# A sorted segment sum by one-hot matrices: three of eight regular one-hots made by GpSimd

## The chip, the cores and the metric

The kernel runs on one core of a Trainium2 chip. The metric is the device time of one execution in microseconds; for the kernel before, three runs were timed. A core has five engines that run side by side and wait for each other through semaphores: TensorE (PE), VectorE (DVE), ScalarE (ACT), GpSimd (POOL) and SyncE (SP), which here only issues DMAs.

## The reference, cut to what matters

One layer of a graph network over 50,000 nodes of 128 values and 25,000 edges, whose targets `dst` are sorted (and crowd at the low node numbers, since they are drawn as 50,000 u²):

```python
h = jnp.maximum(_layernorm(x, axis=-1), 0.0)
msg_input = jnp.concatenate([h[src], h[dst], edge_attr], axis=-1)
x1 = jax.nn.relu(msg_input @ Wm1 + bm1)
messages = jax.nn.relu(x1 @ Wm2 + bm2)
agg = jax.ops.segment_sum(messages, dst, num_segments=N)
u = jax.nn.relu(jnp.concatenate([h, agg], axis=-1) @ Wu1 + bu1)
out = x + h + (u @ Wu2 + bu2)
```

## The kernel before, in words

**Two parts.** The first part (to about 532 us) normalises the nodes, gathers the two ends of each edge and makes `msgs`, the messages already multiplied by their half of `Wu1`, in tiles of 128 edges. It also leaves two scratch tensors in HBM, the rest of the hidden input (`hu_scratch`) and x + h + bias (`xh_scratch`). The second part, which the change is about, goes over 98 groups of 512 nodes. For each group it sums the messages that end in it, and writes 512 rows of the result.

**The sum of a group.** A table `ranges` tells, for each group g, the range of edge tiles that touch it: at least two, so there are always two regular tiles (the first, n = 0, and the second, n = 1) and, in the early groups, some more. For each tile the kernel needs a one-hot matrix `hot` of 128 edges by 512 nodes (1 where `node` equals `dst` minus the group's base), and the messages split in two parts that TensorE takes exactly: `high` (ScalarE rounds it) and `low` = message - `high` (GpSimd subtracts). TensorE adds `low` x `hot` and `high` x `hot` into the group's bank (L871, L872).

**Who makes the one-hots.** The program text goes through the groups in fours; `slot` is g mod 4, and slot s uses the buffers 2s and 2s + 1 of `hot`, `high` and `low` for its regular tiles. VectorE makes the one-hot of the first tile of every group, and of all further tiles (L769). The one-hot of the second tile comes from ScalarE in slots 0, 1 and 2, in two activations: `dist` = |node - place| (L832) and `hot` = relu(1 - `dist`) (L839). For that GpSimd makes `place`, a column of `dst` minus base (L753). In slot 3 VectorE makes both. So of eight regular one-hots of four groups VectorE makes five and ScalarE three.

**Order on each engine.** Each engine runs its own instruction stream in program order; `EdgeTiles.visit` (L165) has the order within a group: the ranges of the next four groups are loaded into registers in slot 0 (L171), then comes what stands in `before` (GpSimd's place), then the first regular tile, the further tiles, and the second regular tile.
- ScalarE, group g: `high` of the first tile, of further tiles, `dist`, `high` of the second, `hot`, and then `u_t` = relu(`hu_i`) of group g - 2 (L856). It begins a group when the sum of g - 4 is done.
- GpSimd, group g: `place` (L753, slots 0 to 2), then a `low` part (L739) for each tile, as the `high` parts come.
- VectorE, group g: its one-hots, then `hu_i` += the sum of g - 2 (L792), then `xh_o` = output bank + `xh_i` of g - 4 (L803).
- TensorE, group g: the output product of g - 3 (L905), then the sums of g.
- SyncE: loads of `hu_i` and `xh_i` up to four groups ahead (L131, L134) and the store of the result (L717), 256 KB each.

## Time and profile before

| What | Value |
|---|---|
| Median of three runs | 800.0 us (798.3 to 801.7) |
| Profiled execution | 800.3 us |
| Its span, first to last instruction | 798.4 us |
| Granted TensorE clock | 0.998 |
| Busy over the span: PE, DVE, ACT, POOL | 87%, 85%, 79%, 71% |
| Second part, from the first sum to the end | about 532 to 798 us |

The times of single instructions are those of the one profiled execution. The busy shares above are means over both parts, which have different limits: GpSimd's 71% is mostly the issuing of gathers in the first part, and says nothing of the room that it has in the second. For the change the stretches of the second part have to be read one by one.

### The profile page before, as it was taken

What the parts mean: (1) busy time and instruction counts of PE and PEld (TensorE: products, weight loads), DVE (VectorE), ACT (ScalarE), POOL (GpSimd) and SP (SyncE); (2) the same over time, 40 slices, a digit from 0 to 9 for tenths busy, and PEclk for the clock granted to TensorE, in tenths of its full rate; (3) what the DMA queues carried; (4) which work ended last, traced back from release to release, by engine and by line L of the source; (5) the groups of instructions that cost most, each with busy time, mean ns of one, the idle gap of its engine ahead of it and who ended that gap; (6) DMA issues with size and microseconds to landing.
All of it is one profiled execution on the core that took longest, in us unless ns stands there. A gap on an engine that the chain in (4) does not pass through costs nothing.

```text
span 798.4 us, 18682 instructions
## 1 busy us (share of the span) xinstructions
PE 694.5 (87%) x3154; PEld 414.7 (52%) x3155; DVE 676.5 (85%) x2269; ACT 630.5 (79%) x1434; POOL 563.7 (71%) x784
## 2 busy tenths in 40 slices
PE   0398999999988888888888888889999999999997
PEld 0244444444444444434444444445778778776765
DVE  2798888988888888888888888769999998998886
ACT  0588888888888888888888888756788888888886
POOL 7777777777777777777777777639777656655542
PEclk9999999999999999999999999999999999999999
DMA  5466666666666666666666665450579999999998
GB/s 153 119 212 217 215 217 220 228 223 216 217 217 208 199 205 213 213 209 201 199 203 210 213 217 184 149 211 14 172 228 271 335 339 330 368 346 348 360 355 292
DMA packets 99727, 184.56 MB, mean 231 GB/s; under 512 B 15101, under 2 KB 16512, under 8 KB 99700
## 3 DMA queue, kind: packets, MB, share of 16 engines
q1 hardware_dynamic: 46628, 81.69, 30.5%
q10 hardware_dynamic: 40528, 76.89, 26.9%
q0 software_dynamic: 12544, 25.72, 12.0%
q14 instruction: 21, 0.17, 0.1%
q8 instruction: 6, 0.10, 0.0%
HBM read 107.25 MB, written 76.98 MB: 231 GB/s over the span
## 4 chain that ended last, share of the span: by engine, by line
DMA 38%; PE 20%; issue 19%; DVE 7%; POOL 6%; ACT 4%; DVEq 2%; ACTq 2%; SPq 1%; POOLq 1%
DMA xg<-x_in,ends_all 36%; PE bank L871 7%; PE bank L905 5%; POOL xg L318 5%; PE bank L872 5%; DVE hot L769 2%; ACT zn L506 1%; DVE xg L446 1%; DVE hu_i L792 1%; DVE xh_o L803 1%; ACT high L823 1%; ACT dist L832 1%; POOL low L739 1%; DVEq L171 1%; DMA hu_i<-hu_scratch 1%
## 5 line engine op out<-in xcount | busy, mean ns | idle before, releaser
L318 POOL DMA_INDIRECT xg<-x_in,ends_all x392 | 392.9, 1002 | 119.9 <-DMA xg<-x_in,ends_all 104.5
L739 POOL TENSOR_TENSOR low<-msgs,high 128x128 fp32r<-128x128 f32 x303 | 153.0, 520 | 88.1 <-ACT high L823 84.2
L506 ACT ACTIVATE zn<-xn,shift,rstd 128x128 f32<-128x128 f32 x392 | 160.5, 483 | 2.0 <-DVE shift L423 1.8
L871 PE MATMUL bank<-hot,low 128*128 128x512 f32 x303 | 136.1, 449 | 10.3 <-DVE hot L769 3.9
L769 DVE TENSOR_SCALAR hot<-node,dst_f,minus_base 128x512 fp32r<-128x512 f32 x229 | 131.3, 619 | 15.6 <-PE bank L872 11.7
L381 DVE BATCH_NORM_STATS2 bn<-xg 128x6 f32<-128x128 f32 x392 | 80.5, 278 | 51.8 <-DMA xg<-x_in,ends_all 51.8
L872 PE MATMUL bank<-hot,high 128*128 128x512 f32 x303 | 119.6, 395 | 0.0
L609 PE MATMUL bank<-ident,xg 128*128 128x128 f32 x392 | 64.5, 288 | 54.8 <-DVE xg L446 54.8
L625 PE MATMUL bank<-ht,w_uh 128*128 128x512 f32 x196 | 106.1, 623 | 2.9 <-ACT ht L525 1.9
L446 DVE TENSOR_SCALAR xg<-xg,rstd,shift 128x128 f32<-128x128 f32 x392 | 107.3, 357 | 0.1
L905 PEld LDWEIGHTS bank<-w_out,u_t 128*128 128x128 f32 x784 | 99.1, 191 | 15.4 <-issue 7.1
L905 PE MATMUL bank<-w_out,u_t 128*128 128x128 f32 x784 | 105.5, 278 | 0.7 <-ACT u_t L856 0.7
L823 ACT ACTIVATE high<-msgs 128x128 fp32r x303 | 81.8, 299 | 20.6 <-issue 10.3
L609 PEld LDWEIGHTS bank<-ident,xg 128*128 128x128 f32 x392 | 41.5, 141 | 106.2 <-DVE xg L446 105.8
L372 DVE BATCH_NORM_STATS2 bn<-xn 128x6 f32<-128x128 f32 x392 | 94.2, 276 | 0.0
L871 PEld LDWEIGHTS bank<-hot,low 128*128 128x128 f32 x303 | 56.9, 188 | 54.4 <-issue 29.5
L525 ACT ACTIVATE ht<-bank,b_u 128x512 f32<-128x512 f32 x98 | 66.5, 678 | 15.5 <-PE bank L625 14.6
L618 PE MATMUL bank<-ident,zn 128*128 128x128 f32 x392 | 52.9, 279 | 29.0 <-ACT zn L506 29.0
L792 DVE TENSOR_TENSOR hu_i<-bank,hu_i 128x512 f32<-128x512 f32 x98 | 66.8, 681 | 6.3 <-PE bank L872 3.9
L856 ACT ACTIVATE u_t<-hu_i 128x512 f32<-128x512 f32 x98 | 60.6, 619 | 12.4 <-DVE hu_i L792 12.3
L803 DVE TENSOR_TENSOR xh_o<-bank,xh_i 128x512 f32<-128x512 f32 x98 | 66.6, 679 | 2.4 <-PE bank L905 1.2
L432 DVE TENSOR_TENSOR xh_o<-zn,xn 128x512 f32<-128x512 f32 x98 | 67.3, 688 | 0.0
(72 smaller groups left out, 1001.8 us busy)
## 6 DMA issues: line engine op xcount, KB each, us to landing
hu_i<-hu_scratch SPq DMA_DIRECT2D x98, 256.0 KB, 4.4
xh_i<-xh_scratch SPq DMA_DIRECT2D x98, 256.0 KB, 4.4
out<-xh_o SPq DMA_DIRECT2D x97, 256.0 KB, 4.4
hu_scratch<-ht ACTq DMA_DIRECT2D x48, 512.0 KB
xh_scratch<-xh_o ACTq DMA_DIRECT2D x48, 512.0 KB
xn<-x_in ACTq DMA_DIRECT2D x44, 512.0 KB, 3.7
xg<-x_in,ends_all POOLq DMA_INDIRECT x392, 2.8
edge<-edge_t_in ACTq DMA_DIRECT2D x45, 64.0 KB
```

The lines of the kernel that those rows point to most:

```text
L318: pool.indirect_dma_start(xg[:, slot, t, :], None, x, bass.IndirectOffsetOnAxis(ap=ends_all[:, s, t:t + 1], axis=0), engine_sem=s_made).th ...
L372: return dve.bn_stats(bn[:, slot % 2, 8 + t, :], xn[:, slot, t, :])
L446: ins = dve.tensor_scalar(xg[:, slot, t, :], xg[:, slot, t, :], rstd[:, half, t:t + 1], shift[:, half, t:t + 1], ALU.mult, ALU.add)
L506: ins = act.activation(zn[:, slot % 2, t - 8, :], xn[:, slot, t - 8, :], ACT.Relu, bias=shift[:, slot % 2, t:t + 1], scale=rstd[:, slot % ...
L609: ins = pe.transpose(p_tr[q][:, j * P:(j + 1) * P], xg[:, slot, 4 * q + j, :], ident[:])
L625: pe.matmul(p_hu[:], w_uh[:], ht[:, slot % 2, 2 + n, :], start=True, stop=True).then_inc(s_hus, 1)
L739: return pool.tensor_tensor(low[:, at, :], msgs[:, k, :], high[:, at, :].bitcast(F32), ALU.subtract)
L769: return dve.tensor_scalar(hot[:, at, :], node[:], dst_f[:, bass.ds(k, 1)], minus_base[:, bass.ds(g, 1)], ALU.subtract, ALU.is_equal)
L823: return act.activation(high[:, at, :], msgs[:, k, :], ACT.Copy)
L871: pe.matmul(to, low[:, at, :], hot[:, at, :], start=start, stop=False, skip_group_check=True)
L872: return pe.matmul(to, high[:, at, :], hot[:, at, :], start=False, stop=stop, skip_group_check=True)
L905: ins = pe.matmul(to[:, j * D:(j + 1) * D], u_t[:, slot % 2, j * P:(j + 1) * P], w_out[:], start=True, stop=True)
```

## The change

Slots 0 and 1 stay as they are (first one-hot by VectorE, second by ScalarE). In slot 2 the second one-hot goes from ScalarE to GpSimd. In slot 3 both one-hots go from VectorE to GpSimd. VectorE now makes three of the eight, GpSimd three and ScalarE two. GpSimd makes a one-hot in one instruction from `node` and a column `place`; it needs two places in slot 3, so `place` has five columns. GpSimd's places in slots 2 and 3 also wait for the sum of g - 4 and for its own one-hots of the round before; a wait for the transposes of the ends is put at the start of its second part.

```diff
-        place, ones = sb("place", [P, 4]), sb("ones", [P, 1])
+        place, ones = sb("place", [P, 5]), sb("ones", [P, 1])
...
+                pool.wait_ge(s_tre, 2 * STEPS)
...
                     def regular(k, at, n):
                         pool.wait_ge(s_hi, 2 * g + n + 1)
+                        if n == 0 and slot > 1:
+
+                            pool.wait_ge(s_rel_p, 3 * use + (1 if slot == 2 else 3))
                         part(k, at).then_inc(s_lo, 1)
+                        if n == 0 and slot > 1:
+                            onehot(2 * slot + 1)
...
-                    def place_of(k):
-                        if slot < 3:
+                    def onehot(at):
+                        pool.tensor_scalar(hot[:, at, :], node[:], place[:, at - 3:at - 2], None, ALU.is_equal
+                                           ).then_inc(s_hot_p, 1)
+
+                    def places_of(k):
+                        def place_of(k, at):
+                            return pool.tensor_tensor(place[:, at:at + 1], dst_f[:, bass.ds(k, 1)],
+                                                      minus_base[:, bass.ds(g, 1)], ALU.add)
+
+                        if slot < 2:
                             if at_least(g, 4):
-                                pool.wait_ge(s_dist, 3 * use + slot - 2)
-                            pool.tensor_tensor(place[:, slot:slot + 1], dst_f[:, bass.ds(k, 1)],
-                                               minus_base[:, bass.ds(g, 1)], ALU.add).then_inc(s_rel, 1)
+                                pool.wait_ge(s_dist, 2 * use + slot - 1)
+                            place_of(k, slot).then_inc(s_rel, 1)
+                            return
+                        if at_least(g, 4):
+                            pool.wait_ge(s_agg, g - 3)
+                            pool.wait_ge(s_hot_p, 3 * use)
+                        if slot == 3:
+                            place_of(k - 1, 3).then_inc(s_rel_p, 1)
+                            pool.wait_ge(s_rel_p, 3 * use + 2)
+                            place_of(k, 4).then_inc(s_rel_p, 1)
+                            onehot(6)
+                        else:
+                            place_of(k, 2).then_inc(s_rel_p, 1)
...
                     def regular(k, at, n):
-                        if n == 0:
+                        if n == 0 and slot < 3:
                             onehot(k, at).then_inc(s_hot, 1)
-                        elif slot == 3:
-                            onehot(k, at).then_inc(s_hot_v, 1)
...
-                        if n == 1 and slot < 3:
+                        if n == 1 and slot < 2:
...
-                        if n == 0:
-                            pe.wait_ge(s_hot, g + 1)
-                        elif slot < 3:
-                            pe.wait_ge(s_hot_a, 3 * use + slot + 1)
+                        if n == 0 and slot < 3:
+                            pe.wait_ge(s_hot, 3 * use + slot + 1)
+                        elif n == 1 and slot < 2:
+                            pe.wait_ge(s_hot_a, 2 * use + slot + 1)
                         else:
-                            pe.wait_ge(s_hot_v, use + 1)
+
+                            pe.wait_ge(s_hot_p, 3 * use + (1 if slot == 2 else 2 + n))
```

How it moves the rows of GpSimd at the start of slot 3 in the loop. Before:

```order
L172 ISA
L739 ISA
L739 TENSOR_TENSOR low<-msgs,high 128x128
L177 REGISTER_ALU
L177 COMPARE_AND_BRANCH
L156 ISA
```

and now:

```order
L172 ISA
L762 ISA
L762 TENSOR_TENSOR place<-dst_f,minus_base 128x1
L767 REGISTER_ALU
L762 ISA
L762 TENSOR_TENSOR place<-dst_f,minus_base 128x1
L757 TENSOR_SCALAR hot<-node,place 128x512
L744 ISA
L747 REGISTER_ALU
L741 ISA
L741 TENSOR_TENSOR low<-msgs,high 128x128
L757 TENSOR_SCALAR hot<-node,place 128x512
```

Two places and a one-hot stand ahead of the first low part of slot 3, and a second one-hot behind it, ahead of everything else in the slot.

ScalarE at the end of slot 2 in the loop (the `else` of further tiles ends with the branch of L179). Before:

```order
L179 UNCONDITIONAL_BRANCH
L829 REGISTER_ALU
L832 ACTIVATE dist<-node,place 128x512
L823 ISA
L823 ACTIVATE high<-msgs 128x128
L839 ACTIVATE hot<-dist,ones 128x512
L853 REGISTER_ALU
L856 ACTIVATE u_t<-hu_i 128x512
```

and now:

```order
L179 UNCONDITIONAL_BRANCH
L846 ISA
L846 ACTIVATE high<-msgs 128x128
L876 REGISTER_ALU
L879 ACTIVATE u_t<-hu_i 128x512
L172 ISA
```

The `dist` and the `hot` around the second high part are gone; nothing else moves.

## Rows read from the trace of the kernel before

**Rows 1.** Busy us (xinstructions) of PE, PEld, DVE, ACT, POOL; clock, DMA share, GB/s

```profile
571.00:595.00 24.00, 22.99 (x119) 17.01 (x119) 23.88 (x43) 17.09 (x48) 18.74 (x39) 1.00 0.76 221
608.00:639.00 31.00, 30.22 (x182) 25.52 (x181) 30.95 (x55) 27.11 (x69) 20.88 (x49) 1.00 0.98 323
684.00:789.00 105.00, 100.81 (x585) 75.03 (x584) 93.41 (x159) 90.61 (x220) 55.27 (x136) 1.00 1.00 353
```

**Rows 2.** Waits, 661 to 787 us: who waited for whom, us, times, longest

```profile
POOL low L739 <- ACT high L823: 45.2, 75, 0.9
```

**Rows 3.** ScalarE's `dist` in four stretches: ns min/median/max, first and last start

```profile
L832 ACT ACTIVATE dist<-node,place x10: 722/724/727, 542.3 to 590.5; 128x512 f32<-128x512 f32 x10
...
L832 ACT ACTIVATE dist<-node,place x13: 707/713/724, 590.5 to 632.6; 128x512 f32<-128x512 f32 x13
...
L832 ACT ACTIVATE dist<-node,place x10: 707/711/723, 632.6 to 661.3; 128x512 f32<-128x512 f32 x10
...
L832 ACT ACTIVATE dist<-node,place x43: 705/710/726, 661.3 to 785.9; 128x512 f32<-128x512 f32 x43
...
  POOL place L753: 11.7, 15
```

**Rows 4.** GpSimd's low parts (L739) alone in the same four stretches, columns as rows 1

```profile
542.31:590.47 48.16, 38.65 (x72) 1.00 0.45 132
590.47:632.58 42.11, 25.70 (x56) 1.00 0.92 290
632.58:661.30 28.72, 15.42 (x33) 1.00 0.98 332
661.30:785.87 124.57, 61.62 (x124) 1.00 1.00 350
```

**Rows 5.** ScalarE in order of time, one late round: start us, us [idle before]

```profile
733.30 0.72 ACT L832 ACTIVATE dist<-node,place 128x512 f32<-128x512 f32 x1 [1.04 <-POOL place L753]
...
736.28 0.71 ACT L839 ACTIVATE hot<-dist,ones 128x512 fp32r<-128x512 f32 x1
736.89 0.62 ACT L856 ACTIVATE u_t<-hu_i 128x512 f32<-128x512 f32 x1
737.41 0.29 ACT L823 ACTIVATE high<-msgs 128x128 fp32r x1
...
739.56 0.49 ACT L823 ACTIVATE high<-msgs 128x128 fp32r x2
...
742.02 0.72 ACT L832 ACTIVATE dist<-node,place 128x512 f32<-128x512 f32 x1 [0.75 <-POOL place L753]
```

**Rows 6.** GpSimd in order of time, the same round

```profile
736.55 0.46 POOL L739 TENSOR_TENSOR low<-msgs,high 128x128 fp32r<-128x128 f32 x1 [0.35 <-ACT high L823]
736.96 0.19 POOL L753 TENSOR_TENSOR place<-dst_f,minus_base 128x1 f32 x1
737.88 0.46 POOL L739 TENSOR_TENSOR low<-msgs,high 128x128 fp32r<-128x128 f32 x1 [0.73 <-ACT high L823]
...
740.02 1.22 POOL L739 TENSOR_TENSOR low<-msgs,high 128x128 fp32r<-128x128 f32 x2 [0.87 <-ACT high L823]
741.80 0.19 POOL L753 TENSOR_TENSOR place<-dst_f,minus_base 128x1 f32 x1 [0.56 <-issue]
```

**Rows 7.** VectorE in order of time: one-hots beside low parts, and alone

```profile
535.69 5.46 DVE L769 TENSOR_SCALAR hot<-node,dst_f,minus_base 128x512 fp32r<-128x512 f32 x9
...
601.35 0.99 DVE L769 TENSOR_SCALAR hot<-node,dst_f,minus_base 128x512 fp32r<-128x512 f32 x2
602.26 0.68 DVE L792 TENSOR_TENSOR hu_i<-bank,hu_i 128x512 f32<-128x512 f32 x1
```

**Rows 8.** GpSimd's groups by line and shape: xcount | busy us, mean ns | idle

```profile
L302 POOL IOTA xh_o<- 128x512 int32 x1 | 0.6, 567 | 0.0
...
L324 POOL TENSOR_SCALAR_AFFINE_SELECT ident<-ident 128x128 f32<-128x128 f32 x1 | 0.3, 304 | 0.0
...
L306 POOL MEMSET eps<- 128x1 f32 x1 | 0.1, 94 | 0.0
```

More of the change, by code:

```diff
@@ L113, in build @@
         s_ldx = [sem(f"xh_loaded{i}") for i in range(4)]
-        s_hot, s_hot_x = sem("first_onehots_ready"), sem("more_onehots_ready")
-        s_hot_a, s_hot_v = sem("last_onehots_by_scalar"), sem("last_onehots_by_vector")
-        s_rel, s_dist, s_one = sem("places_in_group_ready"), sem("distances_ready"), sem("ones_made")
+        s_hot, s_hot_x = sem("first_onehots_by_vector"), sem("more_onehots_ready")
+        s_hot_a, s_hot_p = sem("last_onehots_by_scalar"), sem("onehots_by_gpsimd")
+        s_rel, s_rel_p, s_dist, s_one = sem("places_for_scalar"), sem("places_for_gpsimd"), sem("distances_ready"), sem("ones_made")
         s_hi, s_hi_x = sem("high_parts_ready"), sem("more_high_parts_ready")
@@ L747, in more @@
                         part(k, at).then_inc(s_lo_x, 1)
-                    def place_of(k):
-                        if slot < 3:
-                            if at_least(g, 4):
-                                pool.wait_ge(s_dist, 3 * use + slot - 2)
-                            pool.tensor_tensor(place[:, slot:slot + 1], dst_f[:, bass.ds(k, 1)],
-                                               minus_base[:, bass.ds(g, 1)], ALU.add).then_inc(s_rel, 1)
+                    def onehot(at):
[6 more added lines that the diff above has]
+                        if slot < 2:
+                            if at_least(g, 4):
+                                pool.wait_ge(s_dist, 2 * use + slot - 1)
[11 more added lines that the diff above has]
+                            place_of(k, 2).then_inc(s_rel_p, 1)
                     if not at_least(g, 1):
                         pool.memset(ones[:], 1.0).then_inc(s_one, 1)
-                    tiles.visit(g, slot, regular, more, place_of)
+                    tiles.visit(g, slot, regular, more, places_of)
                 run_steps(pool, GROUPS, 4, GROUPS, 4, body)
@@ L825, in regular @@
                     def regular(k, at, n):
-                        count = 3 * use + slot + 1
-                        if n == 1 and slot < 3:
+                        count = 2 * use + slot + 1
+                        if n == 1 and slot < 2:
                             act.wait_ge(s_rel, count)
@@ L834, in regular @@
                         part(k, at).then_inc(s_hi, 1)
-                        if n == 1 and slot < 3:
+                        if n == 1 and slot < 2:
                             act.wait_ge(s_dist, count)
```

## The prediction

> **What bounds the kernel now.** The stretch that the change touches runs from about 532 us to the end. I first read the engines' busy times by stretch [rows 1]. Up to 639 us VectorE is busy without a break and DMA has room; in 684 to 789 us it is busy 93.4 of 105 us, ScalarE 90.6, GpSimd 55.3, and the DMA engines show a share of 1.00. The granted clock is 1.00 throughout, so TensorE's price per instruction stays out of it. GpSimd looks like the engine with room: it waits for ScalarE's high parts [rows 2].
>
> A share says nothing of who follows whom, so next I read when ScalarE starts the `dist` of slot 0, once in four groups [rows 3]. From 661.3 to 785.9 us lie 43 of them, 14 rounds of four groups (three `dist` each, and the last start is again a slot 0): 124.6 / 14 = 8.90 us a round. The same division gives 28.7 / 3 = 9.57 (632.6 to 661.3), 42.1 / 4 = 10.5 (590.5 to 632.6) and 48.2 / 3 = 16.1 (542.3 to 590.5). The low parts per round are 124 / 14 = 8.9, 11, 14 and 24 [rows 4]; eight of them are regular.
>
> What sets the 8.90 is a ring of two engines. In a late round [rows 5, 6]: `dist` of slot 0 starts at 733.30; ScalarE works through slots 0, 1 and 2 and starts slot 3's high parts at 739.56 (6.26 us on); GpSimd turns these into low parts from 740.02 (0.46 later) in 1.22 us, loads the ranges, makes slot 0's place at 741.80, and `dist` starts at 742.02, having waited 0.75 us for that place. Sum: 6.26 + 0.46 + 1.78 + 0.22 = 8.72, the round's own time. ScalarE waits for the place in all late rounds, 11.7 us in 15 waits [rows 3]. Neither engine is full; the round is a chain that passes through both, and half idle time on GpSimd is its turn to wait.
>
> **The change part by part.** VectorE loses both one-hots of slot 3. Its one-hot costs 0.60 us start to start where GpSimd works beside it (5.46 us for 9) and 0.455 where it doesn't (601.35 to 602.26 for two) [rows 7]. That is 1.1 us a round. It is worth something only up to about 639 us, where VectorE is never idle.
>
> ScalarE loses slot 2's `dist` and `hot`, 0.61 us each start to start: 1.22 us a round. Of the ring this takes a piece: after `dist` of slot 0, slot 2's first high part starts at 737.41 [rows 5], 4.11 us on, and from there GpSimd is what the ring runs through.
>
> GpSimd gains three one-hots and two places a round and gives nothing up. A place is 0.19 [rows 6]. **X, the price of a 128x512 one-hot on GpSimd, is in no row.** Start to start an instruction costs 0.04 to 0.05 less than its row says (low part 736.55, next instruction 736.96, row 0.46). Lower bound: the IOTA of 128x512, which reads nothing, 0.57, so 0.52. Upper bound: a two-input subtraction costs 0.46 at 128 columns and 0.19 at one, 0.27 per 128 columns, so 0.19 + 4 x 0.27 - 0.05 = 1.22. Nearest is the row with one input and a comparison, AFFINE_SELECT of 128x128, 0.304 [rows 8]. With a fixed part of 0.09 (MEMSET of one column) it scales to 0.95, with 0.19 to 0.65; less 0.05, 0.60 to 0.90. I take the middle, 0.75, and 0.05 for the share of SBUF that it must wait for, since VectorE's one-hot beside GpSimd shows such a wait: **X = 0.80**. The Trainium skill (GPSIMD Engine Reference, Elementwise side-by-side cycle accounting) has 769 ns measured for 512 elements in a tight loop with little work per element; the ring's sum would then be 0.1 us a round less. No run here shows that figure yet.
>
> The ring after the change, for four groups of two tiles: from `dist` of slot 0 to slot 2's high part 4.11; to its low part 0.47 (737.41 to 737.88); low part 0.42; one-hot X; low part 0.42; first place of slot 3 with the wait for its own end, 0.34; second place 0.20; one-hot X; low part 0.42; one-hot X; low part 0.42; place of slot 0 and hand-over 0.22. That is 7.02 + 3X = **9.42 us**. The load of the ranges, which stands open today as 0.56 us of idle time ahead of slot 0's place [rows 6], I cost at nothing: it is the sequencer's, and an X and a low part are queued in front of it; without that cover it costs up to 0.56. ScalarE's saved 1.22 us buys nothing in this sum, since ScalarE now waits for the place of slot 0 until GpSimd is through slot 3. Nor can GpSimd begin slot 2 earlier: its one-hots there stand behind a low part that needs ScalarE's high part.
>
> Tiles beyond eight lengthen the ring only where they stand in it: in slot 0 nothing, in slot 1 a high part of 0.2, in slots 2 and 3 a low part of 0.42 (0.5 beside VectorE's one-hots). The mean is 0.26 to 0.30 each. By stretch:
> 661.3 to 785.9: 9.42 + 0.9 x 0.26 = 9.64 against 8.90, x14 = +10.4.
> 632.6 to 661.3: 9.42 + 3 x 0.26 = 10.2 against 9.57, x3 = +1.9.
> 590.5 to 632.6: 9.42 + 6 x 0.3 = 11.2 against 10.5, x4 = +2.8; the first of these rounds holds most tiles and is not longer, so +2.5.
> 542.3 to 590.5: the ring (9.42 + 16 x 0.33 = 14.7) lies under 16.1. VectorE bounds; it gives back 1.1 a round and loses some 0.6 to one-hots of GpSimd in its way, -0.5 in two rounds; the first has no room on GpSimd: -1.0.
> Sum +13.8 us. The profiled execution took 800.3 us (span 798.4) and the median of the three runs is 800.0: 800.3 + 13.8 = **814 us**. Everything ahead of 532 us is untouched; the added wait for the transposes of the ends is over before GpSimd gets its first high part. TensorE now waits for GpSimd's one-hots in slots 2 and 3, but it waits there for the low parts of the same engine anyhow; the last one-hot of slot 3 is ready one low part ahead of its own low part, so no price of its own. GpSimd's added waits for `s_agg` g-3 have nothing behind them that isn't already held by the high parts, since ScalarE waits for the same.
>
> DMA doesn't decide: at 9.6 us a round for four groups it moves less per microsecond than in the 8.9 us of today.
>
> **Rivals.** (a) X is near its lower bound. At 0.55 the late round is 7.02 + 1.65 + 0.23 = 8.90, just today's; below it DMA at its share of 1.00 keeps 8.8 to 8.9. This is the break-even point. With X = 0.52 the total is -2 to 0: 798 to 801. For it: the IOTA row. Against it: AFFINE_SELECT, already half of that at a quarter of the columns. (b) The other side, faster: VectorE is the only bound up to 639 us and the ring has slack that I don't see (ScalarE's saved 1.22 us shortens a path through `u_t`, which in the early rounds is late). Then the seven rounds up to 639 us give back what VectorE loses, up to 1.1 each, until TensorE (30.2 of 31 us busy [rows 1]) stops it: at 0.8 each, -5.6 us: 795. It needs X under 0.6 and half of the one-hots outside VectorE's way. (c) X is dear, near the two-input price, 1.1 to 1.2: 3 x 0.35 x 21 rounds = +22 on top: 836. (d) The one-hots block VectorE for their whole length. Rows show some sharing: 0.60 against 0.455 [rows 7] beside a low part whose row is 0.46 long. If each of three X stops VectorE for 0.8 us, it loses 2.4 where it saves 1.1: +1.3 a round in the five or six rounds that VectorE bounds, and X grows by its waiting: 822. The Trainium skill (SBUF — State Buffer, Who interferes with whom) states just this, an exclusive lock for the whole instruction, taken by whoever issues first. The trace agrees in that both engines slow down together (one-hots 0.60 and low parts about as long in the row of nine); how long a one-hot on GpSimd holds VectorE, no row shows.
>
> **How the numbers follow.** Forecast, X from 0.7 to 0.95, 806 to 820: 0.50. Same mechanism at X from 0.6 to 0.7, 802 to 806: 0.12. (a) 0.12. (b) 0.08. (c) 0.09. (d) 0.09. The range reaches from the upper half of (a), 799, past (d) to the lower part of (c), 828. Over 0.5% is 4 us, about what a measurement of this kernel can tell from no change: slower (over 804) 0.50 + 0.08 + 0.18 = 0.76; same 0.16; faster (under 796) 0.08.
>
> **What would show it.** In the changed kernel's trace: X start to start in the one-hot rows on GpSimd (0.7 to 0.95); the starts of slot 0's `dist` 9.4 to 9.8 us apart late, and ScalarE's wait for the place grown from 0.75 us (today's late round) to about 2.5 us a round, or the same time spent waiting ahead of `u_t`; GpSimd without a gap from slot 2's first low part to slot 0's place; VectorE no longer full before 639 us; DMA's share under 1.00 late. Rounds that stay at 8.9 us with such an X would mean that the chain is cut somewhere, and that I took for a ring what was two engines that only happened to meet.

## The result: 885.7 us, 11% slower, and six times the forecast loss

The changed kernel takes 885.67 us in the median of four runs (882.62 to 890.13), the kernel before, run beside it on the same chip, 800.85 us (798.3 to 802.71). The ratio is 1.107 (95% interval 1.102 to 1.112). Slower was forecast, but by 14 us, not by 85; the time lies far outside the range of 799 to 828 us. Ratios in this text leave out executions over 1.5% longer than the fastest of the same kernel.

The profiled execution took 890.13 us, with a span of 888.3. The page's busy times, and the group of the new one-hots with its durations (ns min/median/max, first and last start):

```profile
PE 726.4 (82%) x3154; PEld 444.0 (50%) x3155; DVE 665.9 (75%) x2221; ACT 605.9 (68%) x1386; POOL 684.4 (77%) x904
...
L757 POOL TENSOR_SCALAR hot<-node,place 128x512 fp32r<-128x512 f32 x72 | 118.2, 1642 | 0.0
...
L757 POOL TENSOR_SCALAR hot<-node,place x72: 1556/1564/1841, 557.2 to 873.6; 128x512 fp32r<-128x512 f32 x72
```

Most of the one-hots on GpSimd are 1.56 us long, 1.53 start to start: twice the X = 0.80 of the forecast, and above its upper bound of 1.22. The mean of all 72 is 1.64, since some are stretched by VectorE's one-hots (see the rivals below). The other engines now have room where they had none. Busy us of PE, PEld, DVE, ACT and POOL, then clock, DMA share and GB/s, of the stretches of [rows 1] and of the late part:

```profile
571.00:595.00 24.00, 20.43 (x100) 16.29 (x99) 18.60 (x32) 13.55 (x39) 20.37 (x37) 0.93 0.55 165
608.00:639.00 31.00, 25.60 (x125) 20.28 (x124) 24.32 (x41) 16.71 (x46) 25.78 (x45) 0.89 0.64 198
700.00:880.00 180.00, 140.43 (x739) 110.66 (x738) 111.87 (x175) 98.79 (x247) 142.89 (x249) 0.92 0.82 258
```

VectorE, full up to 639 us before, works 24.32 of 31 us. Late, DMA has fallen from a share of 1.00 to 0.82. In that late stretch GpSimd is the busiest engine, and even it is idle for a fifth of the time. So there again a chain, and not a full engine, sets the pace. The late `dist` of ScalarE, with what it waited for (compare the last stretch of [rows 3]; there are now two `dist` a round, so 28 steps are 14 rounds), and the waits from 700 to 880 us (us in total, times, longest), which answer to [rows 2]:

```profile
L855 ACT ACTIVATE dist<-node,place x29: 705/721/725, 705.3 to 875.8; 128x512 f32<-128x512 f32 x29
...
  POOL place L762: 51.6, 15
```

```profile
ACT dist L855 <- POOL place L762: 51.6, 15, 4.8
PEld bank L894 <- POOL low L741: 47.9, 43, 2.1
...
POOL low L741 <- ACT high L846: 33.3, 54, 0.8
```

170.5 / 14 = 12.18 us a round against 8.90. ScalarE's wait for slot 0's place has gone from 11.7 to 51.6 us in 15 waits, 3.4 us each. One late round with eight tiles, ScalarE's part of it first, then GpSimd's (start us, us, [idle before]); it answers to [rows 5, 6]:

```profile
804.19 0.72 ACT L855 ACTIVATE dist<-node,place 128x512 f32<-128x512 f32 x1 [4.82 <-POOL place L762]
...
808.30 0.49 ACT L846 ACTIVATE high<-msgs 128x128 fp32r x2
...
815.89 0.72 ACT L855 ACTIVATE dist<-node,place 128x512 f32<-128x512 f32 x1 [3.87 <-POOL place L762]
```

```profile
808.85 0.46 POOL L741 TENSOR_TENSOR low<-msgs,high 128x128 fp32r<-128x128 f32 x1 [0.81 <-ACT high L846]
809.29 1.57 POOL L757 TENSOR_SCALAR hot<-node,place 128x512 fp32r<-128x512 f32 x1
810.82 0.46 POOL L741 TENSOR_TENSOR low<-msgs,high 128x128 fp32r<-128x128 f32 x1
811.23 0.20 POOL L762 TENSOR_TENSOR place<-dst_f,minus_base 128x1 f32 x1
811.60 0.19 POOL L762 TENSOR_TENSOR place<-dst_f,minus_base 128x1 f32 x1 [0.18 <-POOL place L762]
811.76 1.56 POOL L757 TENSOR_SCALAR hot<-node,place 128x512 fp32r<-128x512 f32 x1
813.29 0.45 POOL L741 TENSOR_TENSOR low<-msgs,high 128x128 fp32r<-128x128 f32 x1
813.72 1.56 POOL L757 TENSOR_SCALAR hot<-node,place 128x512 fp32r<-128x512 f32 x1
815.25 0.45 POOL L741 TENSOR_TENSOR low<-msgs,high 128x128 fp32r<-128x128 f32 x1
815.67 0.19 POOL L762 TENSOR_TENSOR place<-dst_f,minus_base 128x1 f32 x1
```

Read as the forecast's ring: 4.11 (804.19 to 808.30) + 0.55 + 0.44 + **1.53** + 0.41 + 0.37 + 0.16 + **1.53** + 0.43 + **1.53** + 0.42 + 0.22 = 11.70 us, the round's own time. The forecast's 7.02 + 3X gives 11.61 with this X. In such a late round the structure was right link by link.

### The profile page after: what moved, and what is told of

It is laid out like the page before. It is cut to its first block, busy times and chain, and to the rows that moved or that the text cites. A ratio compares the mean times of both kernels' runs of the same rounds, so it can differ in the third digit from the quotient of the medians.

```text
span 888.3 us, 18754 instructions
## 1 busy us (share of the span) xinstructions
PE 726.4 (82%) x3154; PEld 444.0 (50%) x3155; DVE 665.9 (75%) x2221; ACT 605.9 (68%) x1386; POOL 684.4 (77%) x904
## 4 chain that ended last, share of the span: by engine, by line
DMA 35%; issue 25%; PE 12%; POOL 10%; ACT 7%; POOLq 5%; DVE 3%; ACTq 2%; SPq 1%; DVEq 0%
DMA xg<-x_in,ends_all 33%; POOL xg L318 4%; POOL low L741 4%; PE bank L894 3%; PE bank L895 3%; ACT high L846 2%; PE bank L929 2%; POOLq L171 2%; ACT dist L855 1%; POOL hot L757 1%; ACT zn L506 1%; ACT u_t L879 1%; POOL place L762 1%; PE bank L609 1%; DMA b_out<-bu_in 1%
## 5 line engine op out<-in xcount | busy, mean ns | idle before, releaser
L318 POOL DMA_INDIRECT xg<-x_in,ends_all x392 | 396.9, 1013 | 119.9 <-DMA xg<-x_in,ends_all 104.5
L894 PE MATMUL bank<-hot,low 128*128 128x512 f32 x303 | 145.2, 479 | 66.9 <-POOL low L741 66.8
L741 POOL TENSOR_TENSOR low<-msgs,high 128x128 fp32r<-128x128 f32 x303 | 148.0, 501 | 61.8 <-ACT high L846 59.7
L794 DVE TENSOR_SCALAR hot<-node,dst_f,minus_base 128x512 fp32r<-128x512 f32 x181 | 110.8, 648 | 46.0 <-PE bank L895 37.7
L895 PE MATMUL bank<-hot,high 128*128 128x512 f32 x303 | 127.5, 421 | 0.0
L381 DVE BATCH_NORM_STATS2 bn<-xg 128x6 f32<-128x128 f32 x392 | 80.5, 276 | 56.9 <-DMA xg<-x_in,ends_all 56.8
L929 PEld LDWEIGHTS bank<-w_out,u_t 128*128 128x128 f32 x784 | 113.9, 212 | 12.2 <-issue 3.6
L894 PEld LDWEIGHTS bank<-hot,low 128*128 128x128 f32 x303 | 62.4, 206 | 112.1 <-POOL low L741 57.2
L757 POOL TENSOR_SCALAR hot<-node,place 128x512 fp32r<-128x512 f32 x72 | 118.2, 1642 | 0.0
L929 PE MATMUL bank<-w_out,u_t 128*128 128x128 f32 x784 | 116.4, 297 | 0.0
L855 ACT ACTIVATE dist<-node,place 128x512 f32<-128x512 f32 x50 | 35.8, 717 | 75.5 <-POOL place L762 74.6
```

Of the source, the lines that this page charges most:

```text
L318: pool.indirect_dma_start(xg[:, slot, t, :], None, x, bass.IndirectOffsetOnAxis(ap=ends_all[:, s, t:t + 1], axis=0), engine_sem=s_made).th ...
L741: return pool.tensor_tensor(low[:, at, :], msgs[:, k, :], high[:, at, :].bitcast(F32), ALU.subtract)
L757: pool.tensor_scalar(hot[:, at, :], node[:], place[:, at - 3:at - 2], None, ALU.is_equal).then_inc(s_hot_p, 1)
L794: return dve.tensor_scalar(hot[:, at, :], node[:], dst_f[:, bass.ds(k, 1)], minus_base[:, bass.ds(g, 1)], ALU.subtract, ALU.is_equal)
L894: pe.matmul(to, low[:, at, :], hot[:, at, :], start=start, stop=False, skip_group_check=True)
L895: return pe.matmul(to, high[:, at, :], hot[:, at, :], start=False, stop=stop, skip_group_check=True)
```

## The experiments

The theory is R: the ring of the prediction, 7.02 + 3X with X = 1.53, so each one-hot costs only what it adds to the chain from slot 2's high part to slot 0's place. Its first rival is P: each one-hot on GpSimd costs its share wherever it stands, since GpSimd, or its access to SBUF, is what is short. Later rivals are named where they come.

The measure is the second part of the kernel, cut by the starts of slot 0's `dist` at groups 0, 12, 28, 40 and 96, which are the four stretches of [rows 3]. This is needed because on the chip that ran e1 to e4, and on that of e10 and e11, the first part took 100 to 130 us longer in every kernel, the one before included (923 and 920 us in all), and by a varying amount (group 0 starts between 645 and 675 us); why was not looked into. What comes after isn't visibly touched by that: e4, whose second part is the code of before, has 242.4 us there and before 243.6. Each sum is of one execution; these two, and e9 and e11 (239.9 and 241.3), which are the same code, show that it repeats to about 1.4 us. The ratio of whole kernels is given too, with that caution for those two chips.

| kernel | 0-12 | 12-28 | 28-40 | 40-96 | sum, us | late round |
|---|---|---|---|---|---|---|
| before | 48.2 | 42.1 | 28.7 | 124.6 | 243.6 | 8.90 |
| after | 60.1 | 58.7 | 38.4 | 170.5 | 327.8 | 12.18 |
| e1_slot2_only | 50.6 | 43.8 | 29.0 | 125.4 | 248.9 | 8.96 |
| e2_slot3_only | 56.9 | 50.8 | 33.4 | 152.1 | 293.2 | 10.86 |
| e3_places_by_vector | 62.0 | 50.8 | 35.7 | 149.6 | 298.1 | 10.69 |
| e5_copy | 51.2 | 46.6 | 29.1 | 132.9 | 259.8 | 9.49 |
| e6_subtract | 56.3 | 52.6 | 33.6 | 150.0 | 292.5 | 10.71 |
| e7_onehot_first | 58.5 | 57.3 | 37.8 | 166.9 | 320.5 | 11.92 |
| e8_scalar_early | 47.0 | 42.0 | 28.0 | 125.6 | 242.6 | 8.97 |
| e9_before_places_by_vector | 48.5 | 42.2 | 28.2 | 121.1 | 239.9 | 8.65 |
| e11_places_again (as e9) | 48.6 | 42.2 | 28.5 | 122.0 | 241.3 | 8.71 |
| e10_both | 47.2 | 42.3 | 28.2 | 122.0 | 239.7 | 8.71 |

In the profiled executions group 0 starts at 542.3 us before and at 547.9 after, and behind group 96 both have 12.5 us. The 5.6 us ahead need not be the change's: e8, with nothing changed there, starts at 546.0 and e7 at 536.0. The second part carries 84.2 of the 89.8 us between the two profiled executions.

**One part alone: e1 and e2.** GpSimd makes slot 2's second one-hot only (e1), or slot 3's two only (e2); the rest is as before.

```
e1:  -  if n == 0 and slot > 1:   onehot(2 * slot + 1)
     +  if n == 0 and slot == 2:  onehot(5)
e2:  +  if n == 0 and slot == 3:  onehot(7)
     (onehot(6) with the places of slot 3, as in the change)
```

> One part of the change alone: GpSimd makes the second one-hot of slot 2 in ScalarE's place; VectorE keeps both of slot 3. One one-hot and one place on GpSimd a round instead of three and three. Theory R (the round is a ring: ScalarE's slots 0 and 1, then GpSimd's slots 2 and 3 up to the place of the next slot 0; an instruction costs only if it stands in the ring): with 1.53 us for the one-hot as the changed kernel's trace has it, the ring is 4.11 + 0.5 + 0.42 + 1.53 + 3 x 0.42 + up to 0.56 for the load + 0.22 = 8.1 to 8.6 us, under the 8.7 to 8.9 of the kernel before; the late round stays at 8.7 to 8.9 (DMA's share is 1.00 there) and the time at 795 to 803 us. Theory P (each one-hot on GpSimd costs its share wherever it stands, since GpSimd or the SBUF port shared with VectorE is what is short): a third of 85 us, 829 us. Theory X0 (it is the dear instruction alone: one one-hot lengthens each of 24 rounds by 1.53 less ScalarE's 1.22): +7 us, 808 us.

> The other part alone: GpSimd makes both one-hots of slot 3 in VectorE's place; ScalarE keeps slot 2. Theory R: ScalarE's slots 0 to 2 stand in the ring again. GpSimd's low part of slot 2's second tile starts 5.4 us after the dist of slot 0; then 0.42, places 0.53, one-hot 1.53, low 0.43, one-hot 1.53, low 0.42, place and hand-over 0.22: a late round of 10.5 us against 8.9, +1.6 in the 17 rounds behind 632 us (+27) and +1 to +1.5 in the seven before them (+8): 830 to 840 us. Theory P (per one-hot): two thirds of 85 us, 857 us.

e1 adds 5.3 us to the second part (ratio 1.023, 1.014 to 1.031), e2 49.6 us (1.065, 1.053 to 1.078); both parts together add 84.2, half as much again as the sum of the two. (The ratio of e1 settles nothing: the medians of all its executions and of before's are 923.99 and 923.01 us.) P expected 28 and 57 us. e1 rules it out as a law for every place: slot 2's one-hot costs 5 us where it is alone and 35 where the two others follow.

R's own sizes were missed, though. It had e1 at no loss; the late round held (8.96 us), but 4.1 of the 5.3 us fall before group 28. (X0 of e1's text, +7 us in all, is near the sum, but puts 4 of it into the last stretch, where 0.8 was measured.) For e2 it had 30 to 40 us and a late round of 10.5; 49.6 and 10.86 came, so that the sum of e2 by itself lies nearer to P. The excess is early here too: 22.1 us up to group 40, where R had about 13. Those stretches come up again below. The late `dist` of both show the reason, each with its wait for the place:

```profile
L848 ACT ACTIVATE dist<-node,place x29: 707/722/726, 774.4 to 899.9; 128x512 f32<-128x512 f32 x29
...
  POOL place L761: 1.7, 4
```

```profile
L851 ACT ACTIVATE dist<-node,place x43: 705/710/725, 786.5 to 938.6; 128x512 f32<-128x512 f32 x43
...
  POOL place L761: 36.7, 15
```

In e1 VectorE makes slot 3's one-hots, and GpSimd's 1.53 us have room in the 0.87 us in which it waited for slot 3's high parts anyway [rows 6] and in the 1.22 us that ScalarE saves. In e2 both one-hots stand between GpSimd's last low part of slot 2 and slot 0's place; in the round that ends at group 96 (933.24 to 938.34 us) GpSimd has no gap there but one of 0.18 us. With all three, slot 2's one pushes the other two back.

**The price itself: e4.** The kernel before, and behind its last group, when all other work is done, GpSimd runs ten forms three times each; their results are not used.

```
+  pool.wait_ge(s_fin, GROUPS)
+  for i in range(3):
+      pool.tensor_scalar(r(), node[:], col, None, ALU.is_equal)
...
+      pool.tensor_tensor(r(), node[:], col.to_broadcast([P, W]), ALU.subtract)
+      pool.tensor_copy(f(), node[:])
```

> The kernel before with 30 further instructions on GpSimd behind its end, when every other engine is done, three of each kind; their outputs are used by nobody. Start to start: tensor_scalar is_equal of 128x512 with a column as scalar, fp32r out (the changed kernel's form). If its 1.53 us is its own price: 1.5 alone too; if it is a wait for SBUF beside VectorE: 0.8 to 1.0 alone. The same at 256 and 128 columns: if it grows by column, about 0.8 and 0.5 (2.9 ns a column), so more a column than the two-input subtraction (2.1 ns). fp32 out instead of fp32r: the same if the output type costs nothing. Immediate scalar instead of a column: the same or less. Subtract instead of is_equal: 0.8 to 1.5; if the compare is what is dear, 0.8. tensor_tensor subtract of 128x512: 1.2 (scaled from 128 columns); with a broadcast column the same. Copy 0.5 to 0.8, affine_select 0.7 to 0.95, as scaled ahead of the prediction. The whole kernel: about 40 us longer than before.

GpSimd in order of time (three instructions a row, so a third of the step from start to start is the price of one):

```profile
906.53 4.67 POOL L773 TENSOR_SCALAR hot<-node,place 128x512 fp32r<-128x512 f32 x3 [4.82 <-DVE xh_o L835]
911.18 4.63 POOL L775 TENSOR_SCALAR msgs<-node,place 128x512 f32<-128x512 f32 x3
915.88 4.59 POOL L777 TENSOR_SCALAR msgs<-node 128x512 f32<-128x512 f32 x3
920.55 4.66 POOL L779 TENSOR_SCALAR msgs<-node,place 128x512 f32<-128x512 f32 x3
925.20 2.72 POOL L781 TENSOR_SCALAR hot<-node,place 128x256 fp32r<-128x256 f32 x3
927.90 1.76 POOL L783 TENSOR_SCALAR hot<-node,place 128x128 fp32r<-128x128 f32 x3
929.63 3.70 POOL L785 TENSOR_TENSOR hot<-node,msgs 128x512 fp32r<-128x512 f32 x3
933.29 3.03 POOL L787 TENSOR_TENSOR hot<-node,place 128x512 fp32r<-128x512 f32 x3
936.27 1.72 POOL L789 COPY msgs<-node 128x512 f32<-128x512 f32 x3
937.96 1.74 POOL L791 TENSOR_SCALAR_AFFINE_SELECT msgs<-node 128x512 f32<-128x512 f32 x3
```

The one-hot costs 1.55 us with nothing beside it, so contention is no part of its price. Neither is its kind: a plain f32 output (1.57), a constant instead of the column (1.56) and a subtraction instead of the comparison (1.55) cost the same. The length counts: 0.90 at 256 columns, 0.58 at 128, about 2.5 ns a column. The form decides: with two whole inputs it is 1.22, with the same column read as a broadcast second input 0.99, copy takes 0.56 and AFFINE_SELECT 0.58. The scaling of the low part's row to 1.22 for a two-input subtraction was exact; what was wrong was to take it for an upper bound of a form with one tile as input.

**The price inside the ring: e5 and e6.** The changed kernel with another instruction in the place of the three one-hots, so that their output holds other numbers (a copy of `node`; a difference instead of a comparison). All waits stay.

```
-  pool.tensor_scalar(hot[:, at, :], node[:], place[:, at - 3:at - 2], None, ALU.is_equal)
e5 +  pool.tensor_copy(hot[:, at, :], node[:])
e6 +  pool.tensor_tensor(hot[:, at, :], node[:], place[:, at - 3:at - 2].to_broadcast([P, W]), ALU.subtract)
```

> The changed kernel with another price in the same three places: GpSimd copies node into hot instead of comparing it (0.57 us start to start in e4 against 1.54); the comparison is left out, so the sums are of other numbers. Places, waits and order stay. Theory R (7.0 us + 3 x price, where that is the longest): 8.6 to 8.9 us a late round, and from the dist of group 0 to that of group 96 about 243 to 248 us, as in the kernel before (243.6) against 327.9 in the changed one. Time within 1% of the kernel before. Theory O (the new waits and the new order, or GpSimd's use of the shared port, cost in themselves, whatever the instruction takes): well above, 270 us or more.

> The same with a third price: tensor_tensor subtract of node and the place column broadcast, 1.00 us start to start in e4; the comparison is left out. Theory R: 7.0 + 3.0 + 0.3 for the tiles beyond eight = 10.3 us a late round, and 280 to 286 us from the dist of group 0 to that of group 96 (a line through 243.6 at 0.55 and 327.9 at 1.53). Theory O: near the changed kernel's 328.

Their 72 instructions in the kernels:

```profile
L757 POOL CAST hot<-node x72: 602/610/862, 547.1 to 796.2; 128x512 fp32r<-128x512 f32 x72
```

```profile
L757 POOL TENSOR_TENSOR hot<-node,place x72: 1032/1040/1349, 549.5 to 830.9; 128x512 fp32r<-128x512 f32 x72
```

With X of 0.57, 1.00 and 1.53 the late round is 9.49, 10.71 and 12.18 us: 2.8 us of round per us of X, near the three of the ring. No other edit lies between the three, so the price is shown to be what most of the loss comes from. A slope near three would come out of a full GpSimd as well; against that stand its idle fifth and ScalarE's waits for the place. R's sizes were missed here too: it had 8.6 to 8.9 us and a sum of 243 to 248 for e5, and 10.3 us and 280 to 286 for e6; 259.8 and 292.5 came, between R and O.

The two runs also measure what the forecast got wrong besides X. A line through e5 and the changed kernel (68.0 us for 0.96 us of X; e6 lies 2 us above it) gives, by an estimate, 276 us for the second part at X = 0.80, +32 where the forecast had +14. So with its own X right it would still have been some 19 us short. Even at 0.57, where the forecast has the break-even, the kernel is slower: 816.64 us against 798.51, ratio 1.024 (1.021 to 1.026). 7.02 + 0.23 for further tiles + 3 x 0.57 is 8.96, and the round is 9.49. One cause stands in GpSimd's rows: the load of the ranges, which I took to be hidden, shows as idle time (0.43 us below) ahead of slot 0's place where little is queued before it. In the 14 late rounds these are 3.5 us in 7 waits, 0.25 a round, so half of the 0.53 that are missing; the rest is open.

```profile
732.78 0.19 POOL L761 TENSOR_TENSOR place<-dst_f,minus_base 128x1 f32 x1 [0.43 <-issue]
```

**Cutting the ring: e3.** The changed kernel with the places of slots 0 and 1, which ScalarE waits for, made by VectorE. GpSimd keeps its one-hots and low parts.

```
-  if slot < 2:
-      place_of(k, slot).then_inc(s_rel, 1)      # GpSimd
+      dve.tensor_tensor(place[:, slot:slot + 1], dst_f[:, bass.ds(k, 1)],
+                        minus_base[:, bass.ds(g, 1)], ALU.add).then_inc(s_rel, 1)
```

> The changed kernel with the ring cut at one place: VectorE makes the places of slots 0 and 1 (two instructions of one column a round), so ScalarE need not wait for GpSimd to finish slot 3. GpSimd still makes all three one-hots. Theory R: the late round falls from 11.7 us to the next longest chain, GpSimd's own work of 8 x 0.42 + 3 x 1.53 + 0.7 = 8.7 or the path from slot 3's one-hot over the sum, u_t and high of slot 2 (about 6.2 + 3.3 = 9.5): 8.9 to 9.8 us, and the time to 825 to 840 us. Theory P (GpSimd's throughput, or the port shared with VectorE): only two places of 0.2 us leave GpSimd, so 11.3 us a round and 877 us or more.

The late round falls from 12.18 to 10.69, so the place was a link that held it (ScalarE's waits for it are down to 2.8 us). But 10.69 lies between R's 8.9 to 9.8 and P's 11.3, and in the first stretch nothing is gained (62.0 against 60.1 us). The waits from 823 to 972 us point to what took its place:

```profile
ACT u_t L881 <- PE bank L931: 30.6, 29, 3.0
PEld bank L896 <- POOL low L741: 30.1, 31, 2.0
...
POOL low L741 <- ACT high L848: 18.4, 24, 2.9
```

ScalarE now waits for TensorE, TensorE for GpSimd's low parts, and those for ScalarE's high parts: read so, a second ring, one engine longer, that runs through the same GpSimd instructions. No run cuts this one. GpSimd itself is busy 128.35 of the 149.60 us from group 40 to group 96, 9.2 us a round, so its own work is not far behind. (The whole-kernel ratio of e3, 1.10 with 1.079 to 1.122, holds a first part that ran 24 to 29 us longer than in e1 and e2.)

**The one-hot of slot 2 one instruction earlier: e7.** In slot 2 the one-hot is put ahead of the regular low parts, right behind its place, where GpSimd waits for the high part (0.81 us in the round above). Behind the wait for that place stands a second `place_of`, 0.16 us, whose value slot 3 overwrites unused; beyond that only waits and their counts change.

```
 def regular(k, at, n):           # behind the low part; waits left out
-    if n == 0 and slot > 1:
+    if n == 0 and slot == 3:
         onehot(2 * slot + 1)
 def places_of(k):                # here slot 2
     place_of(k, 2).then_inc(s_rel_p, 1)
+    pool.wait_ge(s_rel_p, 4 * use + 1)
+    place_of(k - 1, 3).then_inc(s_rel_p, 1)
+    onehot(5)
```

> The changed kernel with one instruction moved: GpSimd makes slot 2's one-hot ahead of the slot's first low part, while ScalarE is still in slot 1, not behind it. For the order of reads and writes it makes one further place (0.16 us). The same work on every engine. Theory R: the one-hot starts 4.19 us after the dist of slot 0 instead of 5.10; the ring is 4.19 + 1.53 + 0.43 + 0.41 + 0.37 + 0.16 + 1.53 + 0.43 + 1.53 + 0.42 + 0.22 = 11.2 us in a round of eight tiles against 11.7, and from the dist of group 0 to that of group 96 about 316 us against 327.8. Theory P (GpSimd's work or the shared port, wherever it stands): no gain, 328 to 332 us.

The second part falls from 327.8 to 320.5 us, in R's direction and by some 60% of what it expected (316); P had no gain. An eight-tile round goes from 844.71 to 856.27, 11.56:

```profile
844.71 0.19 POOL L761 TENSOR_TENSOR place<-dst_f,minus_base 128x1 f32 x1
...
849.11 1.56 POOL L756 TENSOR_SCALAR hot<-node,place 128x512 fp32r<-128x512 f32 x1
850.64 0.87 POOL L741 TENSOR_TENSOR low<-msgs,high 128x128 fp32r<-128x128 f32 x2
851.47 0.38 POOL L761 TENSOR_TENSOR place<-dst_f,minus_base 128x1 f32 x1
...
854.15 1.73 POOL L756 TENSOR_SCALAR hot<-node,place 128x512 fp32r<-128x512 f32 x1
...
856.27 0.18 POOL L761 TENSOR_TENSOR place<-dst_f,minus_base 128x1 f32<-128x1 f32 x1
```

R had 11.2 for such a round. The missing 0.36 us are two links: slot 3's first place takes 0.38 instead of 0.19, and the last one-hot 1.73 instead of 1.56. Each of the two starts while VectorE is in a one-hot (851.26 and 853.88 us), and that adds 0.19 and 0.17.

**The kernel before, used as a test of the forecast's first reading: e8 to e11.** e9 (run again on another chip as e11) is the kernel before with all three places made by VectorE. e8 is the kernel before with ScalarE making slot 3's second one-hot too in the first eight rounds, where VectorE is full. e10 is both.

```
e9:  -  pool.tensor_tensor(place[:, slot:slot + 1], ...)   # GpSimd, slots 0 to 2
     +  dve.tensor_tensor(place[:, slot:slot + 1], ...)
e8:  -  if n == 1 and slot < 3:                 # ScalarE
     +  if n == 1 and (slot < 3 or early[0]):   # early: the first eight rounds
```

> Another way to relieve VectorE where it is the bound: the kernel before, but in the first eight rounds (groups 0 to 31) ScalarE makes all four second one-hots, so VectorE makes four of eight; from group 32 on everything as before. Theory V (up to 639 us VectorE is what bounds, ScalarE has room): 0.5 to 0.6 us a round less in eight rounds, -4 us: 239 us from the dist of group 0 to that of group 96 against 243.6. Rival (the ring through ScalarE is close behind VectorE there, and four pairs of activations lengthen it by 1.22 us): -1 to +3 us.

> The kernel before with its ring cut: VectorE makes the three places (one column each), so ScalarE doesn't wait for GpSimd. Nothing else is changed. If the ring alone sets the late round of 8.9 us, it falls to ScalarE's own 7.8 us or so, but not under what DMA delivers: 8.3 to 8.6 us at 380 to 370 GB/s (the best stretches of the trace of before), -4 to -8 us in 14 rounds. Rival (ring and DMA meet at 8.9 us): no gain late. In the first seven rounds VectorE is the bound and gets three further instructions of 0.15 to 0.25 us: +3 to +5 us. Sum: -5 to +5 us on 243.6 from group 0 to group 96.

> A version meant to beat both kernels: VectorE makes the places (as in the run that cut the ring of the kernel before: 121.1 us from group 40 to group 96 against 124.6), and ScalarE makes all four second one-hots up to group 31 (47.0 us from group 0 to group 12 against 48.2). If the two gains add: 238.5 us from the dist of group 0 to that of group 96 against 243.6, and a ratio of 0.994. If VectorE's places cost in the early rounds what its one-hot saves: 240 us, 0.996 to 1.000.

> The kernel before with the places by VectorE once more, in five rounds, for the size of its gain: 239.9 us from group 0 to group 96 the first time against 243.6 and 242.4; ratio 0.995 to 0.997. If that was chance: 1.000.

With the ring of [rows 5, 6] cut, the late stretch falls from 124.6 to 121.1 (e9) and 122.0 us (e11, e10), and ScalarE no longer waits for a place (no wait in e9's late stretch). So the ring was real in the kernel before, but it had only 0.2 us a round over what bounds next: the late round is 8.65 and 8.71 us, above the 8.3 to 8.6 that e9's text had. What that is, was not told apart; DMA's share is 1.00, and TensorE and VectorE are both at 96%. Busy times from 660 to 770 us in e9:

```profile
660.00:770.00 110.00, 105.74 (x630) 83.48 (x628) 105.41 (x212) 98.25 (x238) 55.01 (x111) 1.00 1.00 357
```

e8 takes 1.2 us off the first stretch and nothing off the second (42.0 against 42.1), and shows 1.0 more in the last one, where its code is that of before; its ratio is 1.001 (0.999 to 1.003), no difference. Theory V had 4 us, so VectorE, though never idle up to 639 us, is not alone in bounding the kernel there: TensorE is busy 22.99 of 24 and 30.22 of 31 us [rows 1]. In e9 the places cost the seven early rounds 0.4 us, not 3 to 5. The sum of e10, 239.7, lies 0.2 us under e9's and 1.6 under e11's, so whether the two gains add (238.5 expected) can't be told. e9 as a whole gives 0.999 (0.994 to 1.005), e11 0.988 (0.978 to 0.998) and e10 0.989 (0.982 to 0.996). The last two hold the long first part. What can be stood for is the second part, 2 to 4 us shorter than before's 243.6 and 1 to 3 than e4's 242.4, at most 0.5%: e9 and e10 are better than the kernel before, if at all, by that.

## Why the prediction was right in direction and wrong in size

**What bounds the kernel, and what replaces it.** Right for the late rounds. The ring was found in the trace of before, e9 confirmed it there (with 0.2 us a round over the next bound), and the changed kernel's late round adds up link by link. That VectorE is the bound up to 639 us is not borne out: e8 relieved it and gained 1.2 us of the 4 expected.

In the first stretch, where the forecast had VectorE as the bound and a gain of 1.0 us, the loss is 12.0 us, and the ring is not what sets it. Before and after (columns as in [rows 1]), and what ScalarE waited for ahead of its seven `dist` there:

```profile
542.31:590.47 48.16, 46.90 (x223) 32.95 (x222) 47.38 (x84) 34.64 (x100) 41.27 (x81) 1.00 0.45 132
...
547.91:608.05 60.14, 49.49 (x216) 35.01 (x215) 45.85 (x77) 32.37 (x94) 54.88 (x97) 0.94 0.38 115
```

```profile
  issue: 0.6, 3
  POOL place L762: 0.2, 1
```

ScalarE waits 0.2 us for a place in all three rounds, and e3, which makes those places elsewhere, is no shorter there. GpSimd, already busy 41.27 of 48.16 us before, has become the busiest engine, with 54.88 of 60.14 us. There its own throughput is the nearest cause, which is theory P; in e5 the nine one-hots there give GpSimd 8.6 us less to do, and the stretch is 8.9 us shorter. This is a reading of busy times; no run takes low parts away from GpSimd.

**X.** This step failed first: "Upper bound: a two-input subtraction", 1.22, and the value 0.80 taken from AFFINE_SELECT, "Nearest is the row with one input and a comparison". The price is 1.53 (alone 1.55, in the mean of the kernel 1.61). The number of inputs and the kind of operation turned out to be no guide at all between forms of instruction on GpSimd: of forms that read one tile, AFFINE_SELECT and copy cost 0.56 to 0.58 and TENSOR_SCALAR 1.55. The same scaling that was exact for TENSOR_TENSOR was carried over to a form of which the trace had no row. The figure of the Trainium skill (GPSIMD Engine Reference, Elementwise side-by-side cycle accounting), 769 ns for 512 elements as the best case of a tight loop, is half of what this form takes here, and that page's section Engine selection, by which one-input work runs at roughly line rate, holds here for the copy (0.57) and not for TENSOR_SCALAR, which is dearer than the two-input form. The measurement decides.

With X = 1.53 in it, the forecast's own sum gives 14 x 11.84 + 3 x 12.39 + 4 x 13.4 + 3 x 16.9 = 307 us for the second part, +64 against 243.6: 864 us. So X accounts for 50 of the 70 us that the sum was short.

**The rest of the sum.** Mis-sized, the other 20 us: 9 in the first stretch, 5 in each of the second and the last, 1 in the third. Part of it is X once more: 72 one-hots at 0.08 us above 1.53 are 6 us. In the first stretch the forecast's tiles stand in a ring that isn't what bounds; every low part is work of the engine that is nearly full. In the other stretches the tiles beyond eight were priced too low. I had 0.26 to 0.30 us each, on the ground that those of slots 0 and 1 cost little or nothing. Against the eight-tile round of 11.70 they come to (12.18 - 11.70) / 0.9 = 0.53, (12.8 - 11.7) / 3 = 0.37 and (14.7 - 11.7) / 6 = 0.50 us a tile, about what a low part takes; but 11.70 is the shortest of the six eight-tile rounds behind 700 us (11.70 to 12.12, mean 11.86), and against the mean the last stretch gives 0.36. That the tiles of the first two slots count too is worked out, and was not tried by an experiment of its own.

**VectorE's and ScalarE's gains.** ScalarE's 1.22 us bought nothing, as forecast: it waits 3.4 us a round. VectorE's relief was to give 1.0 us back in the first stretch; it gave nothing, since VectorE is no longer the bound there (18.60 busy of 24 us). e8, which relieves VectorE early without giving GpSimd a one-hot, shows what there was to be had: 1.2 us.

**The load of the ranges.** Costed at nothing with the cover that an X gives: right in the changed kernel, where no idle time stands there, and wrong once X is small (0.25 us a round in e5).

**Rivals.** (a) had the wrong break-even: at X = 0.57 the kernel already loses 16 us in the second part (259.8 against 243.6). (b) fell with X. (c) was the right mechanism, but its own bound of 1.2 was below the price, and its 836 us with it. (d), one-hots that block VectorE for their whole length, is not borne out. VectorE beside GpSimd's one-hots of 811.76 and 813.72 us (rows above) and of 825.59 us:

```profile
812.18 0.55 DVE L794 TENSOR_SCALAR hot<-node,dst_f,minus_base 128x512 fp32r<-128x512 f32 x1 [1.70 <-PE bank L895]
...
813.87 0.82 DVE L794 TENSOR_SCALAR hot<-node,dst_f,minus_base 128x512 fp32r<-128x512 f32 x1
...
826.42 0.53 DVE L794 TENSOR_SCALAR hot<-node,dst_f,minus_base 128x512 fp32r<-128x512 f32 x1
```

```profile
825.59 1.82 POOL L757 TENSOR_SCALAR hot<-node,place 128x512 fp32r<-128x512 f32 x1
```

All three start and end inside a one-hot of GpSimd; what counts is how far in. The one that starts 0.15 us in takes 0.82 us and leaves GpSimd's at 1.56. The one 0.42 us in takes 0.55, as with nothing beside it (0.53), and GpSimd's stays at 1.56. The one 0.83 us in takes 0.53, and GpSimd's grows to 1.82. The other starts in this trace follow suit: where GpSimd's one-hot itself was not held up, those 0.09 to 0.41 us in all end about 0.97 us after its start; those from 0.58 to 0.83 us in leave VectorE at 0.53 to 0.55, and GpSimd's takes 1.59 to 1.84. So each holds the other up, but, read so, GpSimd's blocks VectorE only in its first part and not for its whole length. The Trainium skill (SBUF — State Buffer, Who interferes with whom) has the pair taken for the whole instruction, where VectorE runs in a mode that uses both ports; no run shows which mode this one-hot runs in, and on GpSimd's side the measured hold is shorter. The forecast's 0.05 us on X was right for a round with no VectorE one-hot under way when GpSimd's starts; where one is, it is 0.17, and up to 0.3 in other positions.

## What to carry to other kernels

Before work is moved to another engine, look for a row of exactly that instruction form there, and where there is none, say that its price is open rather than bound it by forms that look alike: on GpSimd the forms with 512 columns spread from 0.56 to 1.55 us, and the one chosen was the dearest. An engine with half its time idle may be half of a ring: follow one round from the start of an instruction to its next start, and ask between which two links the new work stands. In the late rounds the same 1.5 us cost next to nothing in one slot of this kernel (e1) and most of their length in the next (e2). And read each stretch by itself: early on, the same engine was simply close to full.

## What the runs showed of the hardware

On GpSimd, TENSOR_SCALAR (one tile and a column or constant) costs 1.55 us at 128x512, more than TENSOR_TENSOR on two tiles (1.22) and than TENSOR_TENSOR with the same column as a broadcast (0.99). Written in that last way the changed kernel's ring would have been 1.5 us a round shorter (e6: 292.5 us, still 49 above before); e6 does so with a subtraction, and the comparison was not tried in that form.

TensorE's granted clock, 1.00 throughout the second part before, was 0.93, 0.89 and 0.92 in the three stretches shown above, a mix of its 2.4 and 1.2 GHz levels. In the late stretch, through which it kept falling to the lower level and coming back, TensorE stood waiting for GpSimd's low parts again and again, 47.9 us in 43 waits, none longer than 2.1 us. The 128x512 matmuls of L895 took 420 ns in the mean there, against 396 before. Their part in the loss is small: what the late round has over 7.02 + 0.23 + 3X is 0.53 us in e5 and 0.46 in e6, at a whole-kernel clock of 0.997 and 0.995, and 0.34 in the changed kernel.
